# Scores and exponential of the next query tile issued before the second half of P·V, and the quantizer's statistics split around the output step

## The chip, the cores and the metric

The kernel runs on all 8 cores of one Trainium2 chip, each with its own program copy and its own data. The metric is the device time of the slowest core in microseconds. Three runs of the kernel before took 724.16, 725.63 and 728.30 us; the median is 725.63 us.

## The reference

One pre-norm transformer layer on x of shape (4, 4096, 1024), with an attention of rank 64 and a feed-forward step with quantized weights and activations:

```
h  = layernorm(x)
P  = softmax((h Q^T)(h K^T)^T / 32)          # Q, K: 64 x 1024
x  = x + P (h VO)                            # VO: 1024 x 1024
g  = layernorm(x)
w_scale = mean|W| + 1e-8 ;  w_quant = clip(round(W / w_scale), -1, 1)
a_scale = max|g| + 1e-8  (per row) ;  a_quant = round(clip(g / a_scale * 127, -128, 127))
x  = x + (a_quant w_quant^T) * (w_scale * a_scale / 127)
```

## The kernel before, in words

Each core takes one half of the 4096 rows of one batch element as its queries (16 tiles of 128 rows) and all 4096 rows of it as keys and values (32 tiles). There is no traffic between cores.

The first stage (lines 343 to 374, up to about 247 us) normalizes the 32 tiles, transposes them on TensorE, and makes V, the key and query projections, and the ternary weights `wqT`. The change does not touch it.

The second stage is a loop over the 16 query tiles t, one pass for each, written out by hand. A small scheduler (`Sched.emit`) appends every operation to the list of its engine in the order of the calls, and adds waits on semaphores for what the operation reads and overwrites. So each engine runs its own list in the order of the calls in the loop; nothing is reordered afterwards. The steps and what they put on which engine:

- `stA1a(t+1)`: the load of the residual tile (SP, L382) and score matmul 0 (TensorE, L385). `stA1b0(t+1)`: score matmul 1 (TensorE, L419). Both write `ps_s01`.
- `stA1ne(t+1)`: a negated maximum over the first 128 scores (VectorE, L395), then the exponential of scores 0 to 1023 into `Pbf` with its sum (ScalarE, L399), which needs that maximum as its bias.
- `stA1b1(t+1)`: 8 transposes of the first group of `Pbf` (TensorE, L453) and their copy to `PT` (ScalarE, L458); score matmuls 2 to 7 (L419), of which 4 and 5 write `ps_kq`, each pair followed by an exponential (ScalarE, L431).
- `stB_tp(t)`: the other three groups of transposes and copies, each interleaved with 8 matmuls of P·V for output columns 0 to 511 (L467). `stB_pv(t, 1)`: 32 matmuls of P·V for columns 512 to 1023 (L467).
- `stC1r(t)`: reciprocal of the softmax sum (VectorE, L492, L495). `stC1h(t, eh)`: attention output of one half plus residual (L503) and its statistics (L510), on VectorE. `stC1a2(t)`: mean and variance (VectorE, L518 to L524), then logarithm and exponential for 1/sigma (ScalarE, L527, L529).
- `stC1b(t)`: subtract the mean (L537), maximum of the absolute value (L541), three small dependent operations (L544, L548, L550), the scaled tile `yp` (L555) and a small product (L559), all VectorE.
- `stC2(t)`: rounding by successive comparison, 17 passes of VectorE over 128 x 1024 elements (L565 to L581), ending in `aq`.
- `stD_tp(t-1)`: 8 transposes of `aq` of the tile before (TensorE, L592), two copies to `aqT` (ScalarE, L598). `stD_ffn(t-1)`: 16 matmuls into `ps_kq` (TensorE, L609). `stD_out(t-1)`: two operations that scale and add the residual (VectorE, L626), and the store (GpSimd's queue, L636).

Of the kernel before, what the change touches and what calls it, by code (L numbers as in the profile page):

```python
# [67 lines left out]
def build_nc(nt=32, nq=16):  # L68
# [12 lines left out]
    with es:  # L81
        def sb(name, shape, dt=F32):
            return es.enter_context(nc.sbuf_tensor(name, shape, dt))
# [34 lines left out]
        st2 = [sb(f"st2{p}", [128, 32]) for p in range(2)]  # L118
# [272 lines left out]
        def stA1ne(t):  # L391
            par = t % 2
            stp = st2[par]
            stok = [f"st2{par}_{k}" for k in range(28)]
            S.emit("vector", lambda e, stp=stp: e.reduce_max(  # L395
                out=stp[:, 0:1], in_=ps_s01[:, 0:128], axis=AX, negate=True),
                reads=["ps_s01_0"], writes=[stok[0]])
            def expp(e, par=par, stp=stp):
                return e.activation(out=Pbf[:, 0:1024],  # L399
                                    in_=ps_s01[:], func=AF.Exp,  # L400
                                    bias=stp[:, 0:1],
                                    accum_out=easum[:, 8 * par:8 * par + 1])
            S.emit("scalar", expp,
                   reads=["ps_s01_0", "ps_s01_1", stok[0]],
                   writes=["P0", "P1", f"easum{par}_0"])
# [33 lines left out]
        def stA1b0(t):  # L439
            for c in range(min(2, NKC)):  # L440
                _a1b_chunk(t, c)

        def stA1b1(t):
            _tp_group(t, 0)
            for c in range(2, NKC):
                _a1b_chunk(t, c)
# [15 lines left out]
        def _pv_group(t, g, eh):  # L462
            def pvmm(e, g=g, eh=eh):
                last = None
                for sl in range(8):
                    kb = 8 * g + sl
                    last = e.matmul(  # L467
                        ps_a[eh], PT[:, 128 * kb:128 * kb + 128],
                        V[:, 1024 * kb + 512 * eh:1024 * kb + 512 * eh + 512],
                        start=(kb == 0), stop=(kb == nt - 1))  # L470
                return last
            S.emit("tensor", pvmm,
                   reads=[f"PT{g}"] + [f"V{8 * g + sl}e{eh}" for sl in range(8)],
                   writes=[f"ps_a{eh}"])

        def stB_tp(t):
            for g in range(1, ng):
                _tp_group(t, g)
                _pv_group(t, g - 1, 0)
            _pv_group(t, ng - 1, 0)  # L480

        def stB_pv(t, eh):
            if eh == 0:
                return
            for g in range(ng):
                _pv_group(t, g, eh)

        def stC1r(t):
            par = t % 2
            stp = st2[par]  # L490
            stok = [f"st2{par}_{k}" for k in range(28)]
            S.emit("vector", lambda e, stp=stp, par=par: e.reduce_sum(  # L492
                out=stp[:, 1:2], in_=easum[:, 8 * par:8 * par + NKC // 2], axis=AX),
                   reads=[f"easum{par}_{c}" for c in range(NKC // 2)], writes=[stok[1]])
            S.emit("vector", lambda e, stp=stp: e.reciprocal(out=stp[:, 2:3], in_=stp[:, 1:2]),  # L495
                   reads=[stok[1]], writes=[stok[2]])

        def stC1h(t, eh):
            par = t % 2
            stp = st2[par]  # L500
            stok = [f"st2{par}_{k}" for k in range(28)]
            def hop(e, eh=eh, par=par, stp=stp):
                return e.scalar_tensor_tensor(  # L503
                    out=hb[par][:, 512 * eh:512 * eh + 512], in0=ps_a[eh],
                    scalar=stp[:, 2:3], in1=xres[par][:, 512 * eh:512 * eh + 512],
                    op0=OP.mult, op1=OP.add)
            S.emit("vector", hop, reads=[f"ps_a{eh}", stok[2], f"xres{par}"],
                   writes=[f"hb{par}_{eh}"])
            def bno(e, eh=eh, par=par, stp=stp):
                return e.bn_stats(out=stp[:, 3 + 6 * eh:9 + 6 * eh],  # L510
                                  in_=hb[par][:, 512 * eh:512 * eh + 512])
            S.emit("vector", bno, reads=[f"hb{par}_{eh}"], writes=[stok[3 + eh]])
# [16 lines left out]
            S.emit("scalar", lambda e, stp=stp: e.activation(out=stp[:, 20:21], in_=stp[:, 19:20], func=AF.Exp, scale=-0.5),  # L529
                   reads=[stok[19]], writes=[stok[20]])  # L530

        def stC1b(t):
            par = t % 2
            stp = st2[par]
            stok = [f"st2{par}_{k}" for k in range(28)]
            def uop2(e, par=par, stp=stp):
                return e.tensor_scalar_add(out=hn[par][:], in0=hb[par][:],  # L537
                                           scalar1=stp[:, 17:18])
            S.emit("vector", uop2, reads=[f"hb{par}_0", f"hb{par}_1", stok[17]],
                   writes=[f"hn{par}"])  # L540
            S.emit("vector", lambda e, par=par, stp=stp: e.reduce_max(  # L541
                out=stp[:, 21:22], in_=hn[par][:], axis=AX, apply_absolute_value=True),
                reads=[f"hn{par}"], writes=[stok[21]])
            S.emit("vector", lambda e, stp=stp: e.tensor_scalar(  # L544
                out=stp[:, 22:23], in0=stp[:, 21:22], scalar1=stp[:, 20:21],
                scalar2=1e-8, op0=OP.mult, op1=OP.add),
                reads=[stok[21], stok[20]], writes=[stok[22]])
            S.emit("vector", lambda e, stp=stp: e.reciprocal(out=stp[:, 26:27], in_=stp[:, 22:23]),  # L548
                   reads=[stok[22]], writes=[stok[26]])
            S.emit("vector", lambda e, stp=stp: e.tensor_scalar(  # L550
                out=stp[:, 23:24], in0=stp[:, 26:27], scalar1=stp[:, 20:21],
                scalar2=127.0, op0=OP.mult, op1=OP.mult),
                reads=[stok[26], stok[20]], writes=[stok[23]])
            def ypop(e, par=par, stp=stp):
                return e.tensor_scalar(out=yp[par][:], in0=hn[par][:],  # L555
                                       scalar1=stp[:, 23:24], scalar2=0.5,
                                       op0=OP.mult, op1=OP.add)
            S.emit("vector", ypop, reads=[f"hn{par}", stok[23]], writes=[f"yp{par}"])
            S.emit("vector", lambda e, stp=stp: e.tensor_tensor(  # L559
                out=stp[:, 24:25], in0=stp[:, 22:23], in1=bcast2[:, 1:2], op=OP.mult),  # L560
                reads=[stok[22], "bcast2"], writes=[stok[24]])
# [58 lines left out]
        def stD_out(t):  # L620
            par = t % 2
            stp = st2[par]
            stok = [f"st2{par}_{k}" for k in range(28)]
            for eh in range(2):
                def oop(e, eh=eh, par=par, stp=stp):
                    return e.scalar_tensor_tensor(  # L626
                        out=outb[par][:, 512 * eh:512 * eh + 512],
                        in0=ps_kq[:, 512 * eh:512 * eh + 512],
                        scalar=stp[:, 24:25],
                        in1=hb[par][:, 512 * eh:512 * eh + 512],  # L630
                        op0=OP.mult, op1=OP.add)
                S.emit("vector", oop, reads=[f"ps_kq_{eh}", stok[24],
                                             f"hb{par}_{eh}"],
                       writes=[f"outb{par}_e{eh}"])
            def stx(e, t=t, par=par):
                return e.dma_start(out=y[128 * t:128 * (t + 1), :], in_=outb[par][:])  # L636
            S.emit("gpsimd", stx, reads=[f"outb{par}_e0", f"outb{par}_e1"],
                   sem=f"do{par}", dma=True)
# [5 lines left out]
        for t in range(nq):  # L644
            stB_tp(t)
            stC1r(t)
            stC1h(t, 0)
            stB_pv(t, 1)
            if t + 1 < nq:
                stA1a(t + 1)  # L650
                stA1b0(t + 1)
            stC1h(t, 1)
            if t > 0:
                stD_tp(t - 1)
            stC1a2(t)
            if t > 0:
                stD_ffn(t - 1)
            if t + 1 < nq:
                stA1ne(t + 1)
            stC1b(t)  # L660
            if t > 0:
                stD_out(t - 1)
            if t + 1 < nq:
                stA1b1(t + 1)
            stC2(t)
# [33 lines left out]
def get_nc(nt=32, nq=16):  # L699
    key = (nt, nq)  # L700
    if key not in _NC_CACHE:
        _NC_CACHE[key] = build_nc(nt, nq)
    return _NC_CACHE[key]
# [23 lines left out]
```

How the kernel before makes its waits and increments, by code:

```python
            def body(eng):  # L677
                for waits, fn, sem, step in S.ops[name]:
                    for psem, pv in waits:
                        eng.wait_ge(sems[psem], pv)
                    inst = fn(eng)
                    inst.then_inc(sems[sem], step)
                if name == "gpsimd":
                    for sn, val in final_waits:
                        eng.wait_ge(sems[sn], val)
```

## Time and profile before

| what | value |
|---|---|
| median of 3 runs | 725.63 us |
| the profiled execution's own time | 725.49 us |
| span in its profile (slowest core, core 7) | 723.7 us |
| spans of the 8 cores | 711.5 to 723.7 us |
| TensorE matmul busy | 571.6 us (79%) |
| VectorE busy | 509.2 us (70%) |
| ScalarE busy | 260.4 us (36%) |
| GpSimd busy | 9.3 us (1%) |

The span is the time from the first to the last instruction of the core; the execution's own time is 1.8 us longer. The busy shares are means over both stages; the page's slices show VectorE at 8 to 9 tenths from the sixteenth slice on, which is the loop, and at 1 to 6 tenths before it. The rows of a timeline are instructions in order of their start. Each begins with start and duration in microseconds, then engine, line, operation, output and input, and in brackets how long the engine had been idle before and what released it.

### The profile page before, as it was taken

Reading aid. Unit: us, or ns where it says so; the run is one execution under the profiler, and the core shown is the slowest. Engines: PE = TensorE matmul, PEld = TensorE weight load, DVE = VectorE, ACT = ScalarE, POOL = GpSimd, SP = SyncE. Lnnn points to the kernel's source line nnn. Section 1 sums busy time; section 2 is a strip of 40 time slices with the busy share of each in tenths; the row PEclk is TensorE's granted clock in tenths of the full one; section 3 lists DMA queues with packets and bytes.
Section 4 is the critical chain, followed back from the end, with each engine's and each line's share of the span. In section 5 each row is a group of like instructions: output and inputs, shape, how many; then the busy total and the mean of one; then the engine's idle time right before and its main releaser. Section 6 shows DMA issues by size and latency. Waiting matters only on the chain.

```text
span 723.7 us, 9675 instructions; the slowest of 8 cores (711.5 to 723.7 us)
## 1 busy us (share of the span) xinstructions
PE 571.6 (79%) x3284; PEld 278.0 (38%) x3284; DVE 509.2 (70%) x824; ACT 260.4 (36%) x491; POOL 9.3 (1%) x22
## 2 busy tenths in 40 slices
PE   1179998678687898898798798897897897988803
PEld 1045554333343443344344344343343343443301
DVE  4124444446665118898898898898898898888883
ACT  1435676232332514414325225225234234244100
POOL 0000000000000000000000000000000000000000
PEclk9999999788988988999989999998999999989966
DMA  4613564332234000101101001001001001000000
GB/s 158 216 63 117 175 194 133 111 115 91 88 117 145 1 1 30 58 1 59 39 20 59 29 30 59 29 30 60 29 30 59 29 30 59 29 30 30 0 29 29
DMA packets 12880, 47.27 MB, mean 65 GB/s; under 512 B 1440, under 2 KB 1440, under 8 KB 12832
## 3 DMA queue, kind: packets, MB, share of 16 engines
q1 hardware_dynamic: 10528, 38.28, 16.2%
q0 software_dynamic: 2304, 8.39, 2.9%
q8 instruction: 26, 0.43, 0.2%
q14 instruction: 22, 0.18, 0.1%
HBM read 38.27 MB, written 8.39 MB: 64 GB/s over the span
## 4 chain that ended last, share of the span: by engine, by line
PE 40%; DVE 35%; issue 10%; DMA 9%; ACT 3%; DVEq 1%; SPq 1%; POOL 0%; ACTq 0%; POOLq 0%
PE ps_a L467 19%; DVE sbuf_s L578 10%; PE ps_a L302 9%; DMA wstg<-ww 6%; DVE cbuf L574 5%; DMA wstg<-vo 3%; DVE st L541 3%; DVE hb L503 2%; PE ps_t L453 2%; PE ps_kq L609 2%; PE ps_t L286 2%; DVE aq L279 2%; DVE outb L626 2%; DVE hn L537 2%; PE ps_kq L318 1%
## 5 line engine op out<-in xcount | busy, mean ns | idle before, releaser
L467 PE MATMUL ps_a<-V,PT 128*128 128x512 bf16 x1024 | 244.0, 396 | 1.4 <-ACT PT L458 1.4
L467 PEld LDWEIGHTS ps_a<-V,PT 128*128 128x128 bf16 x1024 | 102.2, 102 | 121.4 <-issue 19.1
L302 PE MATMUL ps_a<-VOc,xnT 128*128 128x512 bf16 x512 | 129.9, 411 | 19.8 <-ACT VOc L168 18.3
L578 DVE TENSOR_TENSOR sbuf_s<-sbuf_s,cbuf 128x1024 f32<-128x1024 f32 x112 | 137.2, 1225 | 11.6
L574 DVE TENSOR_SCALAR cbuf<-sbuf_s 128x1024 f32<-128x1024 f32 x112 | 77.7, 694 | 12.6 <-DVE sbuf_s L569 0.5
L458 ACT COPY PT<-ps_t 128x1024 bf16<-128x1024 bf16 x64 | 64.5, 1011 | 58.9 <-PE ps_t L453 58.9
L302 PEld LDWEIGHTS ps_a<-VOc,xnT 128*128 128x128 bf16 x512 | 52.2, 105 | 84.6 <-issue 39.4
L598 ACT COPY aqT<-ps_t 128x512 bf16<-128x512 bf16 x32 | 17.2, 589 | 183.3 <-PE ps_t L592 183.3
L279 DVE TENSOR_SCALAR aq<-xstg,st 128x1024 bf16<-128x1024 f32 x32 | 25.9, 810 | 68.3 <-ACT st L270 33.7
L609 PE MATMUL ps_kq<-wqT,aqT 128*128 128x512 bf16 x256 | 65.8, 416 | 9.4 <-ACT aqT L598 9.4
L312 ACT CAST V<-ps_a 128x512 bf16<-128x512 f32 x64 | 34.3, 588 | 72.3 <-PE ps_a L302 72.3
L453 PE MATMUL ps_t<-ident,Pbf 128*128 128x128 bf16 x512 | 44.7, 238 | 12.1 <-ACT Pbf L399 11.9
L453 PEld LDWEIGHTS ps_t<-ident,Pbf 128*128 128x128 bf16 x512 | 36.4, 107 | 36.9 <-issue 29.6
L291 ACT COPY xnT<-ps_t 128x1024 bf16<-128x1024 bf16 x32 | 32.3, 1009 | 40.9 <-PE ps_t L286 40.7
L609 PEld LDWEIGHTS ps_kq<-wqT,aqT 128*128 128x128 bf16 x256 | 25.8, 105 | 44.3 <-issue 22.6
L286 PE MATMUL ps_t<-ident,aq 128*128 128x128 bf16 x256 | 23.6, 246 | 22.2 <-DVE aq L279 22.2
L419 PE MATMUL ps_kq<-xkT,xqT 64*128 64x512 bf16 x32 | 13.1, 421 | 28.8 <-DVE outb L626 28.7
L431 ACT ACTIVATE Pbf<-ps_s,st 128x1024 bf16<-128x1024 f32 x32 | 35.6, 1113 | 0.3 <-PE ps_s L419 0.3
L503 DVE SCALAR_TENSOR_TENSOR hb<-ps_a,st,xres 128x512 f32<-128x512 f32 x32 | 23.8, 742 | 16.7 <-PE ps_a L467 14.4
L592 PE MATMUL ps_t<-ident,aq 128*128 128x128 bf16 x128 | 10.2, 224 | 27.6 <-DVE aq L581 21.5
L419 PE MATMUL ps_s<-xkT,xqT 64*128 64x512 bf16 x80 | 28.4, 422 | 2.0 <-ACT Pbf L431 2.0
L286 PEld LDWEIGHTS ps_t<-ident,aq 128*128 128x128 bf16 x256 | 17.6, 110 | 26.2 <-issue 24.3
(81 smaller groups left out, 467.2 us busy)
## 6 DMA issues: line engine op xcount, KB each, us to landing
xstg<-xb SPq DMA_DIRECT2D x32, 512.0 KB, 3.5
wstg<-ww SPq DMA_DIRECT2D x16, 512.0 KB, 5.5
xres<-xb SPq DMA_DIRECT2D x16, 512.0 KB, 3.3
y<-outb POOLq DMA_DIRECT2D x16, 512.0 KB, 2.9
wstg<-vo SPq DMA_DIRECT2D x8, 512.0 KB, 4.9
xres<-qw SPq DMA_DIRECT2D x1, 256.0 KB, 3.6
xres<-kw SPq DMA_DIRECT2D x1, 256.0 KB, 4.1
```

The source lines that it names most:

```text
L279: return e.tensor_scalar(out=aq[par][:], in0=xstg[par][:], scalar1=stp[:, 14:15], scalar2=stp[:, 17:18], op0=OP.add, op1=OP.mult)
L286: return e.transpose(ps_t[par][:, 128 * j:128 * j + 128], aq[par][:, 128 * j:128 * j + 128], ident[:])
L302: last = e.matmul(ps_a[eh], xnT[par][:, 128 * j:128 * j + 128], VOc[:, 1024 * j + 512 * eh:1024 * j + 512 * eh + 512], start=(j == 0), sto ...
L419: return e.matmul(ap, xqT[0:64, 128 * t:128 * t + 128], xkT[0:64, 512 * c:512 * c + 512], start=True, stop=True)
L431: return e.activation(out=Pbf[:, 1024 * cp:1024 * cp + 1024], in_=tens[:], func=AF.Exp, bias=stp[:, 0:1], accum_out=easum[:, 8 * par + cp: ...
L453: return e.transpose(ps_t[gp][:, 128 * sl:128 * sl + 128], Pbf[:, 128 * kb:128 * kb + 128], ident[:])
L458: return e.copy(out=PT[:, 1024 * g:1024 * (g + 1)], in_=ps_t[gp][:])
L467: last = e.matmul(ps_a[eh], PT[:, 128 * kb:128 * kb + 128], V[:, 1024 * kb + 512 * eh:1024 * kb + 512 * eh + 512], start=(kb == 0), stop=( ...
L503: return e.scalar_tensor_tensor(out=hb[par][:, 512 * eh:512 * eh + 512], in0=ps_a[eh], scalar=stp[:, 2:3], in1=xres[par][:, 512 * eh:512 * ...
L574: S.emit("vector", lambda e, tw=tw: e.tensor_scalar(out=cbuf[:], in0=sbuf_s[:], scalar1=tw, scalar2=tw, op0=OP.is_ge, op1=OP.mult), reads= ...
L578: S.emit("vector", lambda e: e.tensor_tensor(out=sbuf_s[:], in0=sbuf_s[:], in1=cbuf[:], op=OP.subtract), reads=["s_a", "s_b", "cbuf"], wri ...
L609: last = e.matmul(ps_kq[:, 512 * oh:512 * oh + 512], aqT[:, 128 * j:128 * j + 128], wqT[:, 1024 * j + 512 * oh:1024 * j + 512 * oh + 512], ...
```

## The change

In the loop, `stA1a(t+1)` and `stA1b0(t+1)` move ahead of `stB_pv(t, 1)`, and `stA1ne(t+1)`, which stood after `stD_ffn(t-1)`, comes directly behind them, also ahead of `stB_pv(t, 1)`, `stC1h(t, 1)`, `stD_tp(t-1)` and `stC1a2(t)`. `stC1b` is cut in two behind the maximum (L541); `stD_out(t-1)` is called between the two parts.

```diff
-        def stC1b(t):
+        def stC1b_a(t):
...
             S.emit("vector", lambda e, par=par, stp=stp: e.reduce_max(
                 out=stp[:, 21:22], in_=hn[par][:], axis=AX, apply_absolute_value=True),
                 reads=[f"hn{par}"], writes=[stok[21]])
+
+        def stC1b_b(t):
+            par = t % 2
+            stp = st2[par]
+            stok = [f"st2{par}_{k}" for k in range(28)]
             S.emit("vector", lambda e, stp=stp: e.tensor_scalar(
                 out=stp[:, 22:23], in0=stp[:, 21:22], scalar1=stp[:, 20:21],
                 scalar2=1e-8, op0=OP.mult, op1=OP.add),
...
             stC1h(t, 0)
-            stB_pv(t, 1)
             if t + 1 < nq:
                 stA1a(t + 1)
                 stA1b0(t + 1)
+                stA1ne(t + 1)
+            stB_pv(t, 1)
             stC1h(t, 1)
             if t > 0:
                 stD_tp(t - 1)
             stC1a2(t)
             if t > 0:
                 stD_ffn(t - 1)
-            if t + 1 < nq:
-                stA1ne(t + 1)
-            stC1b(t)
+            stC1b_a(t)
             if t > 0:
                 stD_out(t - 1)
+            stC1b_b(t)
             if t + 1 < nq:
                 stA1b1(t + 1)
             stC2(t)
```

## Rows read from the trace of the kernel before

**Rows 1.** Waits between 240 and 720 us: total us, times, longest.
```profile
PE ps_kq L419 <- DVE outb L626: 28.7, 27, 2.3
DVE hb L503 <- PE ps_a L467: 14.4, 2, 9.2
DVE outb L626 <- PE ps_kq L609: 6.6, 1, 6.6
```

**Rows 2.** Timeline, VectorE's instructions of the pass t = 8, and the next start.
```profile
489.15 0.75 DVE L503 SCALAR_TENSOR_TENSOR hb<-ps_a,st,xres 128x512 f32<-128x512 f32 x1
...
490.61 0.73 DVE L503 SCALAR_TENSOR_TENSOR hb<-ps_a,st,xres 128x512 f32<-128x512 f32 x1
...
492.63 0.14 DVE L524 TENSOR_SCALAR st<-st 128x1 f32<-128x1 f32 x1
492.70 0.29 DVE L395 TENSOR_REDUCE st<-ps_s 128x1 f32<-128x128 f32 x1
...
492.91 0.74 DVE L537 TENSOR_SCALAR hn<-hb,st 128x1024 f32<-128x1024 f32 x1
...
493.76 1.22 DVE L541 TENSOR_REDUCE st<-hn 128x1 f32<-128x1024 f32 x1
...
496.74 1.40 DVE L626 SCALAR_TENSOR_TENSOR outb<-ps_kq,st,hb 128x512 f32<-128x512 f32 x2
...
498.06 0.68 DVE L565 TENSOR_SCALAR cbuf<-yp 128x1024 f32<-128x1024 f32 x1
...
515.09 1.23 DVE L581 SCALAR_TENSOR_TENSOR aq<-sbuf_s,yp 128x1024 bf16<-128x1024 f32 x1
...
516.75 0.75 DVE L503 SCALAR_TENSOR_TENSOR hb<-ps_a,st,xres 128x512 f32<-128x512 f32 x1
```

**Rows 3.** The same timeline, TensorE and ScalarE around the feed-forward step.
```profile
488.85 0.61 PE L592 MATMUL ps_t<-ident,aq 128*128 128x128 bf16 x8 [1.12 <-DVE st L492]
...
489.33 1.07 ACT L598 COPY aqT<-ps_t 128x512 bf16<-128x512 bf16 x2 [11.39 <-PE ps_t L592]
...
490.06 3.61 PE L609 MATMUL ps_kq<-wqT,aqT 128*128 128x512 bf16 x16 [0.60 <-ACT aqT L598]
...
493.21 1.10 ACT L399 ACTIVATE Pbf<-ps_s,st 128x1024 bf16<-128x1024 f32 x1
...
494.54 0.61 PE L453 MATMUL ps_t<-ident,Pbf 128*128 128x128 bf16 x8 [0.87 <-ACT Pbf L399]
...
516.64 0.39 PE L385 MATMUL ps_s<-xkT,xqT 64*128 64x512 bf16 x1
```

**Rows 4.** TensorE's timeline of the pass t = 5.
```profile
405.73 0.61 PE L592 MATMUL ps_t<-ident,aq 128*128 128x128 bf16 x8 [1.13 <-DVE st L492]
406.93 5.30 PE L609 MATMUL ps_kq<-wqT,aqT 128*128 128x512 bf16 x16 [0.60 <-ACT aqT L598]
```

**Rows 5.** Busy us by engine in two stretches; behind POOL: granted clock, DMA, GB/s.
```profile
490.06:493.67 3.61, 3.61 (x16) 1.46 (x16) 3.28 (x8) 1.11 (x4) 0.00 (x0) 1.00 0.35 102
...
406.93:412.20 5.27, 5.27 (x19) 2.12 (x20) 4.72 (x10) 1.84 (x5) 0.00 (x0) 0.68 0.31 99
```

**Rows 6.** Timeline, the pass t = 0, which has no output step.
```profile
246.75 0.29 DVE L395 TENSOR_REDUCE st<-ps_s 128x1 f32<-128x128 f32 x1 [4.00 <-PE ps_s L385]
...
247.14 1.11 ACT L399 ACTIVATE Pbf<-ps_s,st 128x1024 bf16<-128x1024 f32 x1
...
274.79 0.21 DVE L544 TENSOR_SCALAR st<-st 128x1 f32<-128x1 f32 x1
...
276.55 0.69 DVE L565 TENSOR_SCALAR cbuf<-yp 128x1024 f32<-128x1024 f32 x1
```

**Rows 7.** Timeline, first L503 of the passes t = 1 and t = 15.
```profile
295.27 0.75 DVE L503 SCALAR_TENSOR_TENSOR hb<-ps_a,st,xres 128x512 f32<-128x512 f32 x1
...
683.07 0.75 DVE L503 SCALAR_TENSOR_TENSOR hb<-ps_a,st,xres 128x512 f32<-128x512 f32 x1
```

**Rows 8.** Timeline, the last feed-forward step and the output step behind it.
```profile
712.14 4.93 PE L609 MATMUL ps_kq<-wqT,aqT 128*128 128x512 bf16 x16 [0.40 <-ACT aqT L598]
...
717.18 1.41 DVE L626 SCALAR_TENSOR_TENSOR outb<-ps_kq,st,hb 128x512 f32<-128x512 f32 x2 [6.59 <-PE ps_kq L609]
```

## The prediction

> **What bounds the kernel now.** The list of waits comes first. From 240 us on, VectorE waited for TensorE's P·V matmuls twice and for the feed-forward matmuls once [rows 1]; both P·V waits lie in the pass t = 0, where no rounding of an earlier tile stands in front, and the other one is the last tile's [rows 8]. In the 14 passes from t = 1 to t = 15, 295.27 to 683.07 us, that is 387.80 us or 27.70 us each [rows 7], VectorE waits for no other engine to speak of, and what it does in order makes the length of a pass. TensorE on the other hand waits for the output step 27 times, 28.7 us [rows 1]: the two score matmuls into `ps_kq` need it to be emptied. So the second view is the timeline of one pass. Call S the start of its first L503. The pass t = 8 has S = 489.15 and the next S is 516.75: 27.60 us [rows 2]. TensorE has finished P·V and issued the next scores before S (516.64 against 516.75, in other passes earlier; in this one it waited 1.12 us for `aq`) [rows 3]. TensorE is thus close behind the path, but not on it, and a gain on its side alone is worth nothing.
>
> Third, what stands around the feed-forward step. `aq` is ready just before S; the transposes start at S - 0.30, the two copies to `aqT` on ScalarE at S + 0.18, the 16 matmuls at S + 0.91, 0.73 us after the first copy, and they end at S + 4.52 [rows 3]. VectorE reads them at S + 7.59, L626 [rows 2]: 3.07 us of slack. That slack is what the change spends.
>
> **Part 1: the exponential goes ahead of the copies.** The call `stA1ne(t+1)` puts L395 on VectorE behind the first half's statistics and L399 on ScalarE, now ahead of the two copies L598, of L527 and L529. ScalarE's list runs in order, so the copies, though their input is ready at S + 0.3, stand behind an exponential that waits for L395; and L395 stands behind the rounding of the tile before. Step by step:
> - L395 takes the place of the second L503, at S + 1.46 [rows 2], and takes 0.29; L399 starts 0.10 after it (247.04 to 247.14 us) [rows 6]: S + 1.85.
> - L399 takes 1.10 [rows 3]: the copies start at S + 2.95 instead of S + 0.18.
> - The matmuls start 0.73 later, S + 3.68 instead of S + 0.91: 2.77 us late.
> - With 3.61 us they end at S + 7.29 [rows 3], and L626 follows 0.11 after their end, as 717.07 to 717.18 us shows [rows 8]: S + 7.40.
>
> The Trainium skill, "TensorE: Matmul & The Clock Gate", section "Architectural detail", says that ScalarE and VectorE are strict first-in-first-out. No row of before shows a ready ScalarE instruction held by a waiting one. By the rule the copies are held; without it they would overtake, and this part would cost nothing.
>
> **Part 2: VectorE's own list.** L395 now costs 0.21 between the halves (492.70 to 492.91 is what it occupies) [rows 2]. Where it stood it hid a dependency: L537 needs L524, which ends at 492.77, and a dependent instruction starts 0.11 after the end of the other (493.65 to 493.76), so at 492.88 instead of 492.91 [rows 2]. Only 0.03 comes back. L541 starts at S + 4.61 + 0.21 - 0.03 = S + 4.79.
>
> The output step now follows L541. L541 takes 1.22, L626 could overlap its end by 0.08: S + 5.93. It has to wait for S + 7.40. Behind it come L626 twice, 1.32 from start to the next instruction (496.74 to 498.06) [rows 2]; L544 to L565, 1.76 (274.79 to 276.55, a pass without L626 between) [rows 6]; L565 to L581, 17.03; L581 to the next S, 1.66 [rows 2]. The pass is 7.40 + 1.32 + 1.76 + 17.03 + 1.66 = 29.17 us. Without the stall it would be 27.70, for moving L626 alone saves 0.07: it fills the gap in front of L544, and L565 no longer stands behind it but 0.1 behind `yp`. So the move forward of L626, which frees `ps_kq` some 1.6 us earlier on paper, is eaten by the late matmuls.
>
> **Part 3: TensorE.** The two score matmuls stand before the second P·V half: it ends later by at most their 0.39 each, by some 0.5 us. In the passes t >= 1 TensorE has more time than that: the pass is longer. At t = 0, where the second L503 waits for P·V, this is on the path: +0.5. The first transposes of `Pbf` no longer wait for the exponential (0.87 us) [rows 3], but then TensorE waits for the output step as before. The load of the residual tile (SP) waits for the same L503 as now, alone in its queue; the output's store leaves GpSimd's empty queue behind L626, nobody waits for it: nothing for both.
>
> **Part 4: TensorE's clock.** The matmuls took 3.61 us at granted clock 1.00 and 5.30 us where the stretch has 0.68 [rows 3 to 5], that is, they ran partly at 1.2 GHz. In that slow case TensorE had waited 1.13 us, transposed for 0.61 and waited 0.60 before them [rows 4]; the pass t = 8 has nearly the same pause and the full clock, so the pause of before is at the edge. Today it costs nothing, as 3.07 us of slack cover 1.69. After the change TensorE does nothing from S + 0.31, the end of the transposes, to S + 3.68. Ahead of the transposes it idles too: the work from L626 to the next S takes VectorE 1.32 + 1.76 + 17.03 + 1.66 = 21.77 us, and TensorE was through 19.9 us after L626 (496.74 to 516.64) [rows 2, 3], so an estimated 1 to 2 us. In all that is some three times the pause of [rows 4]. I expect part of the matmuls at 1.2 GHz in every pass. The bounds are 3.61 (no loss) and twice that, 7.22. I take 5.30; the last tile's, after 21 us idle, took 4.93 [rows 8]. The slack is gone, so each of the 1.69 us counts: 29.17 + 1.69 = 30.86 us.
>
> The same page, section "What's actually happening", says that the throttled state is the default and activity releases it. Taken by itself it would have every group that follows a pause start slow; the group of t = 8 does not. By it the price lies towards the upper bound, the second rival below.
>
> **The sum.** 14 passes: 14 x 30.86 = 432.0 against 387.8, +44.2. Pass t = 0: +0.5. Pass t = 15 has no next tile and no exponential ahead of the copies; with L626 moved ahead of L544 it must wait for matmuls that run slow there, +0.5, or gains 0.1. Together +45. The profiled execution took 725.49 us, 1.8 more than its span, and the median of the runs is 725.63, the same within 0.14. Forecast: 770 us, 6% slower.
>
> **The rivals.**
> - The matmuls keep the full clock: 14 x 29.17 = 408.4, +20.6, and +0.5 for t = 0: 747 us. For it: t = 8 had the full clock after a pause. Against: the pause becomes three times as long. 0.09.
> - All 16 run at 1.2 GHz in each pass: 14 x (29.17 + 3.61) = 458.9, +71 and +1: 798 us. Against: the last group, after 21 us idle, took 4.93 [rows 8]. 0.05.
> - No stall, an even exchange: ScalarE lets the copies pass, or the exponential costs them nothing. Then the pass costs 27.70 against 27.60 in t = 8, +1.5 over 14 passes, +0.5 at t = 0: 727.5 us. 0.03.
> - On the other side: TensorE, not VectorE, sets the pass. If the second P·V half ended later than S + 2.3, the exponential would be over before the copies' input is there, and the earlier L626 would start the next scores 1.6 us sooner: 14 x 1.6 = 22, 703 us. It decides from the point at which P·V ends behind S + 2.3. For it: TensorE's last score starts 0.1 us before S [rows 3]. Against: it ends before S, VectorE waits for it in no pass but t = 0 [rows 1], and a longer pass gives TensorE more room. 0.03.
>
> **How the numbers follow.** The forecast has 0.80. Its own range is 756 to 782: 4.3 to 6.1 us for the matmuls instead of 5.3, 14 us down or 12 up. Below it lie 0.15 for the first, third and fourth rival, above it 0.05. I give 750 to 782, which leaves out these four, 0.20 in all, and takes in some passes with a full clock. Runs of this kernel differ by about 0.5%, 3.6 us, and less can't be told from no change: slower by more than that 0.94, within it 0.03, faster 0.03.
>
> **What would show it.** In a pass of the changed kernel: ScalarE's copies L598 start about 2.9 us behind the first L503 and directly behind L399, with the transposes done 2.6 us before; TensorE waits about 3.4 us for L598; VectorE waits for L609 in front of L626 in 14 passes, 1.5 us if the matmuls take 3.6, about 3.2 if 5.3; passes of 30.9 us; the granted clock at one half at the start of L609. Copies that start at S + 0.2 would overthrow part 1; matmuls of 3.6 us part 4; a wait of L503 for P·V in most passes would say that TensorE is the bound.

## The result and the profile after

The changed kernel takes 771.22 us (median of 10 runs, 768.40 to 772.84), against 725.52 us for the kernel before beside it (10 runs): ratio 1.0627, 95% interval 1.0605 to 1.0648. The forecast was 770 us. The spans of the profiled execution are 759.0 to 769.5 us; before they were 711.5 to 723.7. The ratios, here and below, compare undisturbed executions alone, so that a median can stand a little off its ratio, and profiles are read on undisturbed cores.

The page of the changed kernel: TensorE and VectorE do the same work as before, in a longer span.

```profile
span 769.5 us, 9677 instructions; the slowest of 8 cores (759.0 to 769.5 us)
...
PE 573.4 (75%) x3284; PEld 273.8 (36%) x3284; DVE 511.7 (67%) x824; ACT 257.5 (33%) x491; POOL 9.7 (1%) x22
```

The list of waits from 240 us on: who waited for whom, total us, times, longest. VectorE's output step, L631 now, waits in 14 passes. The wait of L399 for L395 is new, and the feed-forward matmuls (L614) now wait up to 3.5 us for the copies (L603), where they waited 0.6 us before [rows 3]. Before, the output step waited once and the scores for `ps_kq` waited for it 27 times [rows 1]; those waits are gone from the list's head.

```profile
ACT Pbf L399 <- DVE st L395: 205.2, 15, 14.7
...
PE ps_kq L614 <- ACT aqT L603: 45.8, 16, 3.5
DVE outb L631 <- PE ps_t L453: 40.7, 14, 3.5
```

The output step's releaser is named as the transposes L453, which start just before the end of the matmuls L614; what L631 reads is what L614 wrote. These are the lines of one pass, t = 8, that answer to [rows 2, 3]. S is 512.55 here.

```profile
510.89 1.23 DVE L586 SCALAR_TENSOR_TENSOR aq<-sbuf_s,yp 128x1024 bf16<-128x1024 f32 x1
...
512.26 0.82 PE L597 MATMUL ps_t<-ident,aq 128*128 128x128 bf16 x8 [2.33 <-DVE st L492]
...
512.55 0.75 DVE L503 SCALAR_TENSOR_TENSOR hb<-ps_a,st,xres 128x512 f32<-128x512 f32 x1
...
514.01 0.27 DVE L395 TENSOR_REDUCE st<-ps_s 128x1 f32<-128x128 f32 x1
514.20 0.74 DVE L503 SCALAR_TENSOR_TENSOR hb<-ps_a,st,xres 128x512 f32<-128x512 f32 x1
514.38 1.11 ACT L399 ACTIVATE Pbf<-ps_s,st 128x1024 bf16<-128x1024 f32 x1 [14.35 <-DVE st L395]
...
515.49 1.06 ACT L603 COPY aqT<-ps_t 128x512 bf16<-128x512 bf16 x2
...
516.21 5.14 PE L614 MATMUL ps_kq<-wqT,aqT 128*128 128x512 bf16 x16 [3.13 <-ACT aqT L603]
...
517.35 1.22 DVE L541 TENSOR_REDUCE st<-hn 128x1 f32<-128x1024 f32 x1
...
521.45 1.41 DVE L631 SCALAR_TENSOR_TENSOR outb<-ps_kq,st,hb 128x512 f32<-128x512 f32 x2 [2.89 <-PE ps_t L453]
...
543.25 0.75 DVE L503 SCALAR_TENSOR_TENSOR hb<-ps_a,st,xres 128x512 f32<-128x512 f32 x1
```

Read it as a chain. The transposes' results are there at 513.08; ScalarE, idle for 14.35 us, does not take them. It starts L399 when L395 has ended and L603 when L399 has. TensorE idles 3.13 us, the matmuls start at S + 3.66 and end at S + 8.80, and VectorE, done with the maximum at 518.57, stands still until 521.45. The pass takes 30.70 us. The same kernel's stretches, with the columns of [rows 5]: the matmuls, the pause ahead of them, and P.V earlier in the pass.

```profile
516.21:521.35 5.14, 5.14 (x19) 2.12 (x20) 2.14 (x4) 0.64 (x3) 0.00 (x0) 0.70 0.23 92
513.08:516.21 3.13, 0.00 (x1) 0.03 (x1) 2.71 (x7) 1.83 (x4) 0.00 (x0) 0.50 0.14 17
494.42:509.93 15.51, 15.51 (x85) 7.10 (x82) 13.94 (x16) 4.00 (x5) 0.00 (x0) 1.00 0.05 19
```

The granted clock is 1.00 while TensorE works on P.V, 0.50 (1.2 GHz) in the pause and 0.70 over the matmuls: the first part of them runs at half clock.

The difference of the two spans adds up. The 14 passes from t = 1 to t = 15 go from 295.27 and 683.07 us [rows 7] to 296.32 and 727.78 us, 431.46 against 387.80: +43.7. The pass t = 0 is 0.6 longer (32.44 against 31.82) and began 0.4 later. Behind the last S there are 41.7 us against 40.6; the very last matmuls took 5.96 us in this execution, 4.93 before [rows 8]. 43.7 + 0.6 + 0.4 + 1.1 = 45.8 = 769.5 - 723.7.

### The profile page after: what moved, and what is told of

It reads as the page before. It is cut to its first block, busy times and chain, and to the rows that moved or that the text cites. A ratio compares the mean times of both kernels' runs of the same rounds, so it can differ in the third digit from the quotient of the medians.

```text
span 769.5 us, 9677 instructions; the slowest of 8 cores (759.0 to 769.5 us)
## 1 busy us (share of the span) xinstructions
PE 573.4 (75%) x3284; PEld 273.8 (36%) x3284; DVE 511.7 (67%) x824; ACT 257.5 (33%) x491; POOL 9.7 (1%) x22
## 4 chain that ended last, share of the span: by engine, by line
DVE 45%; PE 28%; issue 12%; DMA 9%; ACT 4%; DVEq 1%; SPq 1%; ACTq 0%; POOL 0%; POOLq 0%
DVE sbuf_s L583 18%; PE ps_kq L614 11%; DVE cbuf L579 10%; PE ps_a L302 9%; DMA wstg<-ww 5%; DMA wstg<-vo 3%; DVE sbuf_s L574 3%; PE ps_t L286 2%; PE ps_a L467 2%; DVE outb L631 2%; DVE aq L279 2%; DVE yp L560 2%; DVE hb L503 1%; DVE cbuf L570 1%; PE ps_kq L318 1%
## 5 line engine op out<-in xcount | busy, mean ns | idle before, releaser
L467 PE MATMUL ps_a<-V,PT 128*128 128x512 bf16 x1024 | 233.7, 382 | 0.0
L467 PEld LDWEIGHTS ps_a<-V,PT 128*128 128x128 bf16 x1024 | 97.6, 98 | 113.8 <-issue 9.0
L614 PE MATMUL ps_kq<-wqT,aqT 128*128 128x512 bf16 x256 | 83.1, 497 | 45.8 <-ACT aqT L603 45.8
L399 ACT ACTIVATE Pbf<-ps_s,st 128x1024 bf16<-128x1024 f32 x16 | 17.8, 1114 | 205.3 <-DVE st L395 205.2
L614 PEld LDWEIGHTS ps_kq<-wqT,aqT 128*128 128x128 bf16 x256 | 30.0, 122 | 94.9 <-issue 83.2
L631 DVE SCALAR_TENSOR_TENSOR outb<-ps_kq,st,hb 128x512 f32<-128x512 f32 x32 | 22.6, 746 | 48.3 <-PE ps_t L453 40.7
L453 PE MATMUL ps_t<-ident,Pbf 128*128 128x128 bf16 x512 | 40.2, 223 | 1.6 <-ACT Pbf L399 1.6
L453 PEld LDWEIGHTS ps_t<-ident,Pbf 128*128 128x128 bf16 x512 | 33.3, 99 | 20.5 <-issue 9.5
L419 PE MATMUL ps_s<-xkT,xqT 64*128 64x512 bf16 x80 | 25.9, 389 | 15.4 <-ACT Pbf L431 15.4
L431 ACT ACTIVATE Pbf<-ps_s,st 128x1024 bf16<-128x1024 f32 x32 | 35.9, 1120 | 0.4 <-issue 0.2
L503 DVE SCALAR_TENSOR_TENSOR hb<-ps_a,st,xres 128x512 f32<-128x512 f32 x32 | 23.9, 746 | 15.8 <-PE ps_a L467 7.8
L597 PEld LDWEIGHTS ps_t<-ident,aq 128*128 128x128 bf16 x128 | 9.4, 114 | 64.3 <-issue 64.3
```

Of the source, the lines that this page charges most:

```text
L431: return e.activation(out=Pbf[:, 1024 * cp:1024 * cp + 1024], in_=tens[:], func=AF.Exp, bias=stp[:, 0:1], accum_out=easum[:, 8 * par + cp: ...
L453: return e.transpose(ps_t[gp][:, 128 * sl:128 * sl + 128], Pbf[:, 128 * kb:128 * kb + 128], ident[:])
L467: last = e.matmul(ps_a[eh], PT[:, 128 * kb:128 * kb + 128], V[:, 1024 * kb + 512 * eh:1024 * kb + 512 * eh + 512], start=(kb == 0), stop=( ...
L614: last = e.matmul(ps_kq[:, 512 * oh:512 * oh + 512], aqT[:, 128 * j:128 * j + 128], wqT[:, 1024 * j + 512 * oh:1024 * j + 512 * oh + 512], ...
L631: return e.scalar_tensor_tensor(out=outb[par][:, 512 * eh:512 * eh + 512], in0=ps_kq[:, 512 * eh:512 * eh + 512], scalar=stp[:, 24:25], in ...
```

## The experiments

All times are beside runs of the kernel before on the same chip (its medians 724.7 to 725.4 us). S, "copies", "matmuls" and "output step" are meant as above, for passes t = 1 to 14. Where a mean pass is given, it is the distance from the first L503 of t = 1 to that of t = 15 by 14.

**1. The exponential behind the copies again.** The changed kernel, with the exponential L399 split from its maximum L395 and called after `stD_tp(t-1)` (the comments in the cut are added here).

```diff
+                stA1n(t + 1)        # L395 alone
-                stA1ne(t + 1)
             stB_pv(t, 1)
             stC1h(t, 1)
             if t > 0:
                 stD_tp(t - 1)
+            if t + 1 < nq:
+                stA1e(t + 1)        # L399 alone
```

> The changed kernel with one thing undone: ScalarE's exponential L399 stands behind the two copies to aqT again; the early scores, the early maximum L395 on VectorE and the moved output step stay. Theory A (the copies were held behind the exponential in ScalarE's list, and the feed-forward matmuls with them): copies back at S + 0.2, no wait in front of the output step, passes of 27.7 us, 727 us (725 to 730). Rival B (the early L395 on VectorE, or the scores ahead of the second P.V half, cost the time): stays at 765 to 775. Rival C (the output step in the middle of the statistics costs it): stays there too.

Measured: 734.09 us, ratio 1.0104 (1.0057 to 1.0151). So 37 of the 46 us belong to the exponential's place in ScalarE's list, with everything else of the change kept. Rivals B and C, as causes of the whole, are out. But it is 7 us above the number of theory A. On core 2 the mean pass is 28.23 us instead of 27.7, and the passes are not even: seven of 27.7 to 28.0, and others up to 29.5. One of the long ones:

```profile
430.94 1.01 PE L602 MATMUL ps_t<-ident,aq 128*128 128x128 bf16 x8 [2.64 <-DVE st L497]
...
431.24 0.75 DVE L508 SCALAR_TENSOR_TENSOR hb<-ps_a,st,xres 128x512 f32<-128x512 f32 x1
431.62 1.07 ACT L608 COPY aqT<-ps_t 128x512 bf16<-128x512 bf16 x2 [13.21 <-PE ps_t L602]
...
432.35 6.14 PE L619 MATMUL ps_kq<-wqT,aqT 128*128 128x512 bf16 x16 [0.40 <-ACT aqT L608]
...
438.60 1.41 DVE L636 SCALAR_TENSOR_TENSOR outb<-ps_kq,st,hb 128x512 f32<-128x512 f32 x2 [1.35 <-PE ps_t L458]
```

The copies are back at S + 0.38 (at S + 0.2 or earlier in the ten passes whose transposes ran at full clock). But TensorE waited 2.64 us ahead of the transposes, where it had waited 1.12 [rows 3], and the matmuls took 6.14 us and ran into the output step, which waited 1.35. The output step now comes at S + 5.9 if nothing holds it, not at S + 7.6. The moved output step accounts for both: it lets TensorE finish P.V earlier, into a longer pause, and it takes most of the slack that hid slow matmuls. Experiment 3, which has that move without the early scores, shows the same two things.

**2. The exponential's move alone.** In the kernel before, the three calls `stA1a`, `stA1b0`, `stA1ne` of t + 1 go ahead of `stB_pv(t, 1)`; `stC1b` stays whole, ahead of `stD_out`.

> The first part of the change alone: scores, maximum and exponential early, statistics and output step in the order of before. Theory A: the matmuls start 2.8 us late as in the changed kernel, but the output step is wanted 1.8 us later, at S + 7.77, so the loss is smaller: with matmuls of 5.15 us they end at S + 8.83, wait of about 1.2 us, passes of 28.95 us, 744 us (740 to 748). With matmuls at full clock, S + 7.3, nothing would be lost: 729. Rival C (the moved output step is to blame): 726.

Measured: 751.53 us, ratio 1.0338 (1.0286 to 1.0389). The late matmuls reach the output step although it comes 1.8 us later, as theory A has it, and rival C's 726 is excluded. The size is a miss by 7 us, outside the expected 740 to 748: mean pass 29.76 instead of 28.95. The matmuls start at S + 3.65 in each of the passes t = 1 to 14 and take between 5.0 and 6.5 us, 6.0 in the middle, not 5.15. A pass of it:

```profile
505.98 1.06 ACT L598 COPY aqT<-ps_t 128x512 bf16<-128x512 bf16 x2
506.70 6.45 PE L609 MATMUL ps_kq<-wqT,aqT 128*128 128x512 bf16 x16 [3.34 <-ACT aqT L598]
...
513.26 1.41 DVE L626 SCALAR_TENSOR_TENSOR outb<-ps_kq,st,hb 128x512 f32<-128x512 f32 x2 [2.37 <-PE ps_t L453]
```

How much of the 16 matmuls falls into the slow time changes from pass to pass here (passes of 28.8, 29.7, 30.6 and 30.3 us follow each other, and then similar ones again), while they settled at about 5.1 us in the changed kernel from t = 5 on. One thing that differs is when the clock fell. These are stretches of the pass above, with S = 503.04, and then one of the changed kernel's pass t = 8, with S = 512.55:

```profile
503.00:505.60 2.60, 0.36 (x7) 0.18 (x4) 2.35 (x5) 0.73 (x1) 0.00 (x0) 1.00 0.00 0
505.60:512.50 6.90, 5.80 (x14) 2.05 (x15) 4.44 (x11) 1.74 (x6) 0.00 (x0) 0.51 0.24 76
...
512.55:519.30 6.75, 3.62 (x14) 1.46 (x12) 5.38 (x10) 2.47 (x6) 0.00 (x0) 0.50 0.23 78
```

The half clock holds here from S + 2.6 to S + 9.4 and covers almost all of the matmuls; in the changed kernel it holds from S to S + 6.8, and the last 2 us of the matmuls run at 1.00. Ahead of the transposes TensorE had paused 0.54 us here and 2.33 us there.

Alone, the two parts of the change cost 24.5 us (this one) and 2.5 us (experiment 3) by their ratios, together 45.5. Most of the rest comes from their meeting: the moved output step wants its input 1.8 us earlier in each pass, and 0.7 of that comes back because the late matmuls take 5.2 us on average there and 5.9 here.

**3. The output step's move alone.** The changed kernel with `stA1a`, `stA1b0` and `stA1ne` back in their places of before.

> The second part of the change alone: statistics cut in two with the output step between them, everything else as before. Theory A: matmuls end at S + 4.5, output step wanted at S + 5.7, no wait; it fills VectorE's dependency gap: passes 0.07 us shorter, 724.5 us (723 to 726). Rival C: slower by more than 5 us. A rival that TensorE bounds the passes: the output step frees ps_kq 1.8 us sooner, 14 x 1.8 us, 700 us.

Measured: 728.71 us, ratio 1.0034 (1.0007 to 1.0061): not the small gain expected, but about 2.5 us lost by the ratio. Rival C's loss of more than 5 us and the 700 us of a bounding TensorE are both out. Seven of the 14 passes from t = 1 on take 27.53 to 27.55 us, the 0.07 less of the prediction to within 0.02. In four the matmuls ended late, at S + 6.2 to S + 7.3, and the output step stood waiting, with passes of up to 29.18 us. TensorE's pause ahead of the transposes is 2.4 to 2.7 us in seven of the 14 passes, three of these four among them; in the kernel before it is 1.13 us at most in the same passes. In the kernel before the slow matmuls of t = 5, 6 and 7 end at S + 5.9 to 6.2 too, and the output step at S + 7.6 never noticed.

**4. TensorE kept busy in the pause.** The changed kernel with 14 further matmuls ahead of the feed-forward matmuls, whose results those overwrite.

```diff
+        def stFill(t, n=14):
+            ...  n times e.matmul(ps_kq[:, 0:512], wqT[:, 0:128], V[:, 512 * i:512 * i + 512], start=True, stop=True)
             if t > 0:
+                if t + 1 < nq:
+                    stFill(t - 1)
                 stD_ffn(t - 1)
```

> The changed kernel with 14 more matmuls (128x128 by 512 columns, results overwritten) between the transposes of aq and the feed-forward matmuls, in TensorE's pause of 3.4 us, in the 14 passes that have it. Theory A: the matmuls start as late as before, but the granted clock stays at 1.0 and they take 3.6 instead of 5.1 us: passes of 29.2 to 29.4 us, 748 to 751 us. Rival D (they are slow for another reason than the pause): the clock stays at one half there, 771 us or more.

Measured: 755.95 us, ratio 1.0410 (1.0369 to 1.0452): 15 us less than the changed kernel, though TensorE does more, and 5 us above the range expected. The feed-forward matmuls took 3.6 us in each of the passes t = 1 to 14: rival D is out. Their start was on time, S + 3.66, in three passes only. Two of these took 29.18 and 29.19 us; the third, at 29.55, has one of the delays of 0.3 us that some passes before have too (27.93 instead of 27.60). That is the 29.17 that the prediction gives for a held copy without the clock's part. In the other eleven the clock fell around the transposes, between S - 1.0 and S + 1.0 and behind a pause of 2.3 us in most; the fillers themselves ran slow (4.2 to 4.9 us for 14, instead of 3.19), and the matmuls began at S + 4.5 to 4.9.

**5. The same with the earlier pause filled too.** Eight more fillers ahead of `stD_tp(t-1)`.

> As the kernel with 14 filling matmuls in the changed kernel's pause, with 8 more of them in the pause ahead of the transposes of aq, between the end of P.V and the end of the rounding. There the clock had fallen in 12 of 14 passes, so that the 14 fillers themselves ran at half clock until S + 4.8 and held up the feed-forward matmuls. Theory A: now the clock stays at 1.0 throughout, the matmuls start at S + 3.66 and take 3.61 us in every pass, as in the two passes in which that happened: passes of 29.2 us, 744 us. Rival: the clock falls whatever TensorE does, or TensorE's added work makes it the bound: 756 us or more.

Measured: 749.74 us, ratio 1.0339 (1.0321 to 1.0358), mean pass 29.46. The expectation counts two passes of experiment 4 with the matmuls on time; there are three. In eight of the 14 passes here the matmuls start by S + 3.75, and five of these take 29.17 to 29.19 us. One of them, with S = 559.15 (of 14 fillers ahead of the matmuls the trace has 13):

```profile
556.36 1.89 PE L613 MATMUL ps_kq<-V,wqT 128*128 128x512 bf16 x8
558.86 0.61 PE L597 MATMUL ps_t<-ident,aq 128*128 128x128 bf16 x8 [0.60 <-DVE st L492]
559.30 3.19 PE L613 MATMUL ps_kq<-V,wqT 128*128 128x512 bf16 x13
562.80 3.61 PE L624 MATMUL ps_kq<-wqT,aqT 128*128 128x512 bf16 x16 [0.32 <-ACT aqT L603]
```

The granted clock over the last line's stretch, and over one later in the same pass:

```profile
562.80:566.41 3.61, 3.61 (x19) 1.72 (x20) 2.15 (x4) 0.65 (x3) 0.00 (x0) 1.00 0.37 133
569.54:572.96 3.42, 3.20 (x15) 1.70 (x15) 3.06 (x5) 2.62 (x5) 0.00 (x0) 0.50 0.38 153
```

With the clock kept up over the matmuls, 24 us of the 46 remain: the held copies, and a rest. The rest are the other six passes, in which the fillers came late and held the matmuls up by 0.4 to 0.7 us, 3 us in all. In the pass ahead of each of these six the clock had fallen for a while from S + 10 to S + 12 on, among the scores and P.V, as in the second stretch above, and TensorE was done with P.V that much later. The other 3 us of the miss against 744 lie in the expectation's own sum: 14 passes of 29.2 us instead of 27.7 make 21 us more than before, and with 0.6 for t = 0 that is 747 us, not 744.

**6. The slack by itself.** The kernel before, with the two copies to `aqT` done three times.

```diff
-            for h in range(2):
+            for h in (0, 1, 0, 1, 0, 1):
                 def eva(e, h=h):
```

> The kernel before with the two copies to aqT done three times, so that the feed-forward matmuls start 2 x 1.07 = 2.14 us later in every pass; nothing else. The slack in front of the output step is read as 3.07 us. If the matmuls keep their 3.61 us, they end at S + 6.66, 0.9 us before they are wanted: 726 us, no change. If the longer pause takes the clock down (5.2 us), they end at S + 8.25 and the output step waits 0.8 us: up to 14 x 0.8 = 11, 737 us. A rival by which there is no slack (each us of delay counts): 14 x 2.14 = 30, 756 us.

Measured: 745.63 us, ratio 1.0280 (1.0228 to 1.0331). Neither of the two numbers of theory A, nor the 756 of the rival. The matmuls start at S + 2.87 in most passes, 1.96 us later than in [rows 3] and not the 2.14 meant, as the six copies take 3.03 us together; and none of the 15 passes has them at 3.6 us. They take 4.9 to 6.5 us:

```profile
524.45 3.03 ACT L598 COPY aqT<-ps_t 128x512 bf16<-128x512 bf16 x6 [10.92 <-PE ps_t L592]
...
527.14 4.92 PE L609 MATMUL ps_kq<-wqT,aqT 128*128 128x512 bf16 x16 [2.56 <-ACT aqT L598]
...
532.17 1.41 DVE L626 SCALAR_TENSOR_TENSOR outb<-ps_kq,st,hb 128x512 f32<-128x512 f32 x2 [0.23 <-PE ps_t L453]
```

A delay of 1.96 us does not fit into a slack of 3.07 once the pause it makes costs another 1.3 to 2.9 us. The mean pass is 28.92, 1.2 more than before; a delay with no slack at all would have cost 1.96.

**7. VectorE's rounding in two alternating halves.** On the kernel of experiment 3, each of the rounding operations works on 512 columns, twice, with tokens of their own.

```diff
-            for k in range(6, -1, -1):
-                ... cbuf[:] = (sbuf_s >= tw) * tw        then    sbuf_s[:] -= cbuf
+            for k in range(6, -1, -1):
+                ... cbuf[:, 0:512], cbuf[:, 512:1024]    then    sbuf_s[:, 0:512], sbuf_s[:, 512:1024]
```

> The second part of the change alone, and the 17 rounding operations of VectorE each cut in two halves of 512 columns, alternating, so that a dependent operation no longer follows directly and its 0.11 us gap is filled by the other half. Theory A says VectorE's list makes the pass: if two halves take what the whole takes, 16 gaps of 0.11 to 0.19 us go, 1.8 to 3 us per pass, 690 to 700 us, until TensorE, close behind, becomes the bound. If each half carries 0.06 us of its own, nothing is won: 725. I expect 705. A rival by which VectorE is not the bound: 724.

Measured: 696.08 us, ratio 0.9581 (0.9538 to 0.9625), below both other kernels. The rival's 724 is out, and my 705 was 9 us too high: 0.06 us is what a pair of halves costs more, not each half. Mean pass 25.93. The rounding, one step of seven as the timeline has it:

```profile
485.56 0.76 DVE L584 TENSOR_SCALAR cbuf<-sbuf_s 128x512 f32<-128x512 f32 x2
486.24 1.29 DVE L589 TENSOR_TENSOR sbuf_s<-sbuf_s,cbuf 128x512 f32<-128x512 f32 x2
487.44 0.76 DVE L584 TENSOR_SCALAR cbuf<-sbuf_s 128x512 f32<-128x512 f32 x2
```

A step takes 1.88 us (485.56 to 487.44). Before it took 2.13, 0.69 and 1.23 us of work and two gaps of 0.1, as the seven steps and their frame make up the 17.03 us in [rows 2]. In place of the gaps the next pair starts 0.08 us before the end of the last.

**8. The halves in the order of before.** The kernel before with the halves only.

> The kernel before with the 17 rounding operations in alternating halves, nothing else: order of the output step as before. VectorE's list would allow 25.7 us per pass as in the kernel with the halves and the moved output step (696 us), but the output step frees ps_kq 1.8 us later in the pass, at S + 7.6, and TensorE needs 19.9 us from there to the end of P.V: S + 27.5. Theory: TensorE is now the bound, its second half of P.V is what the second L503 waits for, passes of 26.1 to 26.4 us, 705 us (700 to 709), so that here the early output step is worth something. Rival (VectorE stays the bound, or pauses and clock weigh more than the order): 690 to 697 us, as fast as with the moved output step or faster.

Measured: 694.78 us, ratio 0.9579 (0.9559 to 0.9599): the same as experiment 7 within the intervals, 4.2% faster than before. The theory that TensorE would make passes of 26.1 to 26.4 us is wrong: the mean is 25.85, and six passes of 14 take 25.64, VectorE's own list. TensorE is at the edge, though, for the transposes of `aq` start behind S in all 14:

```profile
524.58 0.75 DVE L503 SCALAR_TENSOR_TENSOR hb<-ps_a,st,xres 128x512 f32<-128x512 f32 x1
...
525.06 0.62 PE L600 MATMUL ps_t<-ident,aq 128*128 128x128 bf16 x8
...
526.28 3.61 PE L617 MATMUL ps_kq<-wqT,aqT 128*128 128x512 bf16 x16 [0.60 <-ACT aqT L606]
```

I had taken the 19.9 us that TensorE needs after the output step from the pass t = 8, in which the scores and the first eight matmuls of P.V had run at half clock.

## Why the prediction was right

**The path.** That VectorE's list makes the pass was right. Experiments 7 and 8 took no work away from any engine, only gaps out of that list, and each pass became 1.8 to 2.0 us shorter.

**Part 1, the hold.** Each step is found where it was put: L395 at S + 1.46 (as predicted), L399 at S + 1.83 (1.85), copies at S + 2.94 (2.95), matmuls at S + 3.66 (3.68). Experiment 1 undoes it and returns 37 us. That ScalarE does not let a ready copy pass a waiting exponential, for which the prediction had only the Trainium skill ("TensorE: Matmul & The Clock Gate", section "Architectural detail"), is shown here: the transposes were done at 513.08 us, ScalarE was idle, and the copies started at 515.49.

**Part 2, VectorE's list.** L541 at S + 4.80 (4.79). The pass without the clock's part, 29.17, occurs in experiments 4 and 5 as 29.17 to 29.19. What failed in this part is "moving L626 alone saves 0.07". It does in seven of 14 passes of experiment 3. The step left out was that L626 moved from S + 7.6 to S + 5.7 has 1.8 us less of slack against slow matmuls, and that TensorE, through earlier, pauses longer ahead of them (2.4 to 2.7 us in half of the passes). Measured: +2.5 us alone instead of -1, and in experiment 1 the 7 us above what the prediction's steps would leave.

**Part 4, the clock.** 5.14 us at t = 8 and 4.9 to 5.7 in the 14 passes, 5.18 on average, against 5.30 taken. The pause ahead of the transposes, estimated at 1 to 2 us, was 2.33. The clock's part was half of the loss per pass: 5.18 - 3.61 = 1.57, beside 29.17 - 27.60 = 1.57 for the hold and the early L395.

That the mean pass of 30.82 us meets the predicted 30.86 so closely is partly luck. The matmuls were put 0.12 us a pass too high. Against that, 29.17 was built from the pass t = 8, which takes 27.60 us, and set against a mean of 27.70, in which four passes of 14 have a delay of 0.3 us; three passes of the changed kernel have it too, 0.08 us on average, and the sum has no term for it.

Experiments 4 and 5 show the cause: work in the pauses, of no use to the result, brings the matmuls back to 3.6 us and makes the kernel up to 21 us faster than without it. The second rival's picture, all 16 matmuls slow in every pass, did not come true.

**The ends.** +0.5 at t = 0 was 0.6. At t = 15 0.1 us was lost: the slow matmuls ended at S + 5.73 and the output step came at S + 5.83, where it comes at S + 5.73 in experiment 7 with fast ones. The last 1.1 us come from the last tile's matmuls. Their 5.96 us instead of 4.93 can't be put down to the change: over the profiles of the eight experiments they take 4.62 to 6.31 us. The 0.4 us by which the loop began later are of the first stage. So 1.5 of the 45.8 us had no term in the sum.

The expectations of experiments 2 and 6 carried 5.15 and 5.2 us over from one kernel to another. The matmuls took up to 6.5 us in these where the half clock covered nearly all of them, as in the stretches of experiment 2, and less where it had begun earlier or was shorter. Why it fell when it did is not settled; the share of the matmuls in the slow time differs from pass to pass, and repeats in experiment 2 after three or four passes.

## What to carry to other kernels

An instruction moved forward is queued ahead of everything that it passes on its engine. Ask what it waits for, and who waits for those behind it: here an exponential of 1.1 us, early by its own needs, held two copies that the next engine was waiting for. Slack that covers a slow case is in use even when the fast case shows it empty: before moving the consumer of a result forward, look at the latest time at which that result was ready in any pass. Where one engine's dependent chain makes the length of a loop, try alternating two independent halves before reordering anything: here that won 4.2%, and the reordering on top of it nothing.

## What the runs showed of the hardware

- ScalarE did not take a ready copy ahead of a waiting exponential: the copies' input was there at 513.08 us, ScalarE was idle, and they started at 515.49, behind the exponential.
- Work added to TensorE's pauses (14, then 22 matmuls a pass) made the kernel faster, 771.2 to 756.0 and 749.7 us, because the matmuls behind them took 3.6 us again, at a granted clock of 1.00. The clock still fell elsewhere in the pass.
- A pause costs again after it has ended: a start 1.96 us later of 16 matmuls made them 1.3 to 2.9 us longer as well (experiment 6).
- Two VectorE operations on 128 x 512 elements, alternating with independent ones, took 0.76 and 1.29 us a pair, where one on 128 x 1024 took 0.69 and 1.23 and left about 0.1 us ahead of each dependent operation. The halves win 0.25 us in 2.13, and the whole kernel 4.2%.
